# A graph network kernel: the count matrix of its sum layers stored by nodes and read in seven fixed pieces

## What is computed

```
# layer 0: attention with edge features
x = layernorm(x + gat_edge(x, src, dst, edge_attr))
# layers 1, 2, 3: for each node, the mean over its incoming edges
agg = segment_sum(x[src], dst, N)
h   = einsum(agg / max(deg, 1), Wl) + bl + einsum(x, Wr)      # relu between them
# layer 4: a sum with degree weights
h   = relu(segment_sum((x @ W.T)[src] * norm[:, None], dst, N) + b)
# layers 5 and 6: attention layers
```

## Time and profile before

| | |
|---|---|
| median of 3 runs | 3435.23 us (3430.89 to 3437.77) |
| profiled execution, whole time | 3430.6 us |
| its span, first to last instruction | 3428.8 us |
| granted PE clock over the span | 0.892 of full speed |
| busy share of the span | PE 81%, PEld 51%, DVE 53%, ACT 37%, POOL 46% |
| four sum layers, first to last matmul of L745 | about 214 us each |
| building the count matrix | about 53 to 271 us |

### The profile page before, as it was taken

How to read it: one execution, slowest core, us unless ns; L and a number is a source line. 1 busy time by engine, 2 the same in 40 slices (tenths; PEclk the granted TensorE clock), 3 DMA queues, 4 the chain that set the end, 5 groups by cost and what they waited for, 6 DMA issues and landing times.

```text
span 3428.8 us, 52282 instructions
## 1 busy us (share of the span) xinstructions
PE 2781.3 (81%) x13349; PEld 1749.2 (51%) x13350; DVE 1822.2 (53%) x4809; ACT 1263.7 (37%) x3238; POOL 1574.4 (46%) x1469
## 2 busy tenths in 40 slices
PE   6887888888889999999998998477667766767665
PEld 4444555555555555556556455345445534545443
DVE  7996998899952000000003002476666636666665
ACT  3664555555532001001004001644444445444445
POOL 5971666666613004004003100467777537777760
PEclk8997999999989999999999999688888778787885
DMA  6336777777712321321330332345555324455541
GB/s 218 119 113 161 209 208 198 204 207 206 208 41 72 103 76 61 101 86 51 102 95 7 109 104 60 101 134 142 138 141 138 107 84 135 138 141 138 141 116 39
DMA packets 238757, 424.50 MB, mean 124 GB/s; under 512 B 53795, under 2 KB 155095, under 8 KB 238335
## 3 DMA queue, kind: packets, MB, share of 16 engines
q1 hardware_dynamic: 163519, 234.32, 22.5%
q0 software_dynamic: 60544, 173.03, 19.1%
q10 hardware_dynamic: 14400, 13.93, 1.4%
HBM read 381.52 MB, written 39.62 MB: 123 GB/s over the span
## 4 chain that ended last, share of the span: by engine, by line
PE 47%; POOL 17%; DVE 15%; issue 12%; DMA 4%; ACT 3%; DVEq 2%; SPq 0%; ACTq 0%; POOLq 0%
PE ps L745 25%; POOL rows L2138 17%; PE ps L629 5%; PE ps L608 4%; DVE norm L1529 3%; PE ps L997 3%; PE ps L977 3%; DMA rows<-table,src_idx 2%; DVE norm L1352 2%; DVE spread L1519 1%; ACT norm L1168 1%; PE ps L915 1%; PE ps L802 1%; PE ps L595 1%; DVE al L1358 1%
## 5 line engine op out<-in xcount | busy, mean ns | idle before, releaser
L2138 POOL DMA_INDIRECT rows<-table,src_idx x1248 | 1360.0, 1090 | 534.1 <-issue 376.0
L745 PE MATMUL ps<-rows,rT 128*128 128x448 f16 (+1 forms) x3200 | 817.1, 342 | 16.6 <-DMA rows<-adjacency 16.6
L745 PE MATMUL ps<-rows,spread 128*128 128x448 f16 (+1 forms) x1600 | 546.6, 342 | 0.0
L745 PEld LDWEIGHTS ps<-rows,rT 128*128 128x128 bf16 x3200 | 312.1, 98 | 278.2 <-issue 25.5
L2092 POOL CAST rT<-rows 128x1024 bf16<-128x1024 f32 (+1 forms) x28 | 26.6, 950 | 783.9 <-ACT rows L1293 783.9
L1545 DVE TENSOR_TENSOR rows<-ps,norm 128x896 f32<-128x896 f32 (+1 forms) x24 | 24.7, 1027 | 667.4 <-PE ps L745 667.4
L802 PE MATMUL ps<-rows,spread 128*128 128x260 f32 x832 | 283.0, 510 | 62.0 <-DVE rows L1660 62.0
L608 PE MATMUL ps<-rT,spread 128*128 128x272 f32 x832 | 248.9, 423 | 68.4 <-DVE norm L1352 67.5
L802 PE MATMUL ps<-rows,w_roots 128*128 128x260 f32 x832 | 263.8, 480 | 41.3 <-DVE rows L1660 41.1
L802 PEld LDWEIGHTS ps<-rows,spread 128*128 128x128 f32 x832 | 211.2, 261 | 117.6 <-DVE rows L1660 63.4
L1660 DVE TENSOR_TENSOR rows<-rows,ps 128x1024 f32<-128x1024 f32 x208 | 249.1, 1198 | 29.6 <-issue 22.0
(11 more groups left out here) (267 smaller groups left out, 4236.5 us busy)
## 6 DMA issues: line engine op xcount, KB each, us to landing
rows<-adjacency SPq DMA_DIRECT2D x140, 560.0 KB, 3.7
rT<-table SPq DMA_DIRECT2D x316, 136.0 KB, 2.5
spread<-in_tiles SPq DMA_DIRECT2D x104, 256.0 KB, 4.1
rows<-table,src_idx POOLq DMA_INDIRECT x1248
rT<-table ACTq DMA_DIRECT2D x100, 136.0 KB
w_table<-in_tiles SPq DMA_DIRECT2D x52, 256.0 KB
adjacency<-rT SPq DMA_DIRECT2D x4, 2800.0 KB, 11.1
adjacency<-acc SPq DMA_DIRECT2D x3, 2800.0 KB, 11.2
```

The source lines that it names most:

```text
L745: ins = mm(chunk_ps[c % 2][:, f, 0:width], xp[k][:, t, f * P:(f + 1) * P], ring[c][q][:, i, :], start=t == 0 and k == 0, stop=t == ROWS - ...
L2138: pool.indirect_dma_start(src_rows(l, par)[:, k, :], None, tables[l][:, :], bass.IndirectOffsetOnAxis(ap=src_idx[:, g * T + k:g * T + k + ...
```

## The change

The matrix gets one array in HBM, by nodes: 128 partitions x 25 rows x 3584 columns, of which 3136 = 7 x 448 are read. A chunk is stored at its first node's column, an address known only at run time, so chunks overlap in HBM and their stores must land in order: SP waits for the store before. Where a chunk begins, PE carries the shared column from the stage of the chunk before (its column is `link`), so that each column's last writer has the whole sum. The sum layers read seven fixed pieces of columns, 448 each, and DVE no longer needs the first node. DVE's preparation works out chunk starts that leave no gap, and `link`. The last chunk is 232 columns wide instead of 200.

```diff
-WIDTHS = [CC] * (NCK - 1) + [200]
+LAST_CHUNK = 232
+COLUMNS = -(-N // CC) * CC
+PIECES = COLUMNS // CC
...
-        adjacency = nc.dram_tensor("adjacency", (NCK * P, ROWS * CC), F16, kind="Internal").ap()
+        adjacency = nc.dram_tensor("adjacency", (P, ROWS, COLUMNS + CC), F16, kind="Internal").ap()
...
-                if j % CP > 0:
-                    shared = pe.value_load(place[0:1, j:j + 1], min_val=0, max_val=CC)
+                if j > 0:
+                    at_first = j % CP == 0
+                    of_stage = adj_stage[(j - 1) // CP % 2]
+                    shared = pe.value_load(link[0:1, j // CP:j // CP + 1] if at_first else place[0:1, j:j + 1], min_val=0, max_val=CC)
                     pe.wait_ge(adj_copied, 2 * j)
...
-            for c in range(NCK):
-                width = WIDTHS[c]
+            for c in range(PIECES):
...
-                                ins = mm(chunk_ps[c % 2][:, f, 0:width], xp[k][:, t, f * P:(f + 1) * P], ring[c][q][:, i, :],
+                                ins = mm(chunk_ps[c % 2][:, f, :], xp[k][:, t, f * P:(f + 1) * P], ring[q][:, i, :],
...
-                if i == 0:
-                    act.wait_ge(key_used, PACK * (j + 1))
+                if j == 0:
+                    act.wait_ge(key_used, PACK)
                 else:
-                    act.wait_ge(carried, (CP - 1) * c + i)
+                    act.wait_ge(carried, j)
...
-                node = V.value_load(chunk_node[0:1, c:c + 1], min_val=0, max_val=NPAD - width)
...
-                nodes = acc[:, :, bass.ds(node, width)]
-                V.tensor_tensor(nodes, nodes, summed, ALU.add).then_inc(window_added, 1)
+                V.tensor_tensor(acc[:, :, of], acc[:, :, of], summed, ALU.add).then_inc(window_added, 1)
...
+                    width = LAST_CHUNK if c == NCK - 1 else CC
+                    node = sp.value_load(chunk_node[0:1, c:c + 1], min_val=0, max_val=COLUMNS)
                     sp.wait_ge(adj_copied, 2 * (CP * c + PACKS_OF[c]))
-                    to = adjacency[c * P:(c + 1) * P, 0:ROWS * WIDTHS[c]].rearrange("p (h c) -> p h c", h=ROWS)
-                    sp.dma_start(to, adj_stage[c % 2][:, :, 0:WIDTHS[c]]).then_inc(adj_stored[c % 2], 16)
+                    if c > 0:
+                        sp.wait_ge(adj_stored[(c - 1) % 2], 16 * ((c - 1) // 2 + 1))
+                    sp.dma_start(adjacency[:, :, bass.ds(node, width)], adj_stage[c % 2][:, :, 0:width]).then_inc(adj_stored[c % 2], 16)
...
-                        piece = HQ * WIDTHS[c]
-                        sp.dma_start(ring[c][q].rearrange("p h c -> p (h c)"),
-                                     adjacency[c * P:(c + 1) * P, q * piece:(q + 1) * piece]).then_inc(piece_landed[q], 16)
+                        sp.dma_start(ring[q], adjacency[:, q * HQ:(q + 1) * HQ, c * CC:(c + 1) * CC]).then_inc(piece_landed[q], 16)
...
+            V.memset(steps_of[:, :], float(CC))
+            V.tensor_copy(firsts[:, :], pack[:, 0:FULL + 1:CP])
+            ch.then(V.tensor_scalar(more_upto[:, 0:NCK], iota[:, 0:NCK], float(CC), float(COLUMNS - LAST_CHUNK - CC * (NCK - 1)), ALU.mult, ALU.add))
+            ch.then(V.tensor_tensor_scan(starts[:, :], steps_of[:, :], firsts[:, :], -float(CC), ALU.add, ALU.min))
+            ch.then(V.tensor_tensor(starts[:, :], starts[:, :], more_upto[:, 0:NCK], ALU.max))
+            V.tensor_copy(chunk_node[:, :], starts[0:1, :])
+            V.memset(link[:, 0:1], 0.0)
+            ch.then(V.tensor_tensor(firsts[0:1, 1:NCK], firsts[0:1, 1:NCK], starts[0:1, 0:NCK - 1], ALU.subtract))
+            V.tensor_scalar(link[0:1, 1:NCK], firsts[0:1, 1:NCK], 0.0, float(CC), ALU.max, ALU.min)
...
-                ch.then(V.tensor_scalar(chunk_node[:, at].unsqueeze(2), first[:, :, 0:1], NPAD - width, None, ALU.min))
...
+                ch.then(V.scalar_tensor_tensor(unfit[:, of], more_upto[:, of], 0.0, unfit[:, of], ALU.is_lt, ALU.add))
```

More of the change, by code:

```diff
@@ L168, in gnn_program @@
         iota16 = sb("iota16", [P, KEYS], F16)
-        chunk_node = sb("chunk_node", [P, NCK], I32)
+        chunk_node = sb("chunk_node", [1, NCK], I32)
+        starts = sb("starts", [P, NCK])
+        firsts = sb("firsts", [P, NCK])
+        steps_of = sb("steps_of", [P, NCK])
+        link = sb("link", [1, NCK], I32)
         place = sb("place", [1, PACKS], I32)
@@ L215, in gnn_program @@
         xp.append(spread[:, :].bitcast(BF16).rearrange("p (t d) -> p t d", t=ROWS))
-        ring = [[rows[:, q * PIECE:q * PIECE + HQ * w // 2].bitcast(F16).rearrange("p (h c) -> p h c", h=HQ) for q in range(NQ)]
-                for w in WIDTHS]
+        ring = [rows[:, q * PIECE:(q + 1) * PIECE].bitcast(F16).rearrange("p (h c) -> p h c", h=HQ) for q in range(NQ)]
         stage_words = [x[:, 0:ROWS * PITCH // 2].rearrange("p (h c) -> p h c", h=ROWS) for x in (low, early)]
@@ L717, in adjacency_pe @@
                         ins = mm(adj_ps[j % 4][:, h, 0:(end - at) * SPAN], lo, hot[:, at * SPAN:end * SPAN],
-                                 start=k == 0, stop=k == PACK - 1 and j % CP == 0)
+                                 start=k == 0, stop=k == PACK - 1 and j == 0)
                     ins.then_inc(key_used, 1)
-                if j % CP > 0:
-                    shared = pe.value_load(place[0:1, j:j + 1], min_val=0, max_val=CC)
+                if j > 0:
+                    at_first = j % CP == 0
+                    of_stage = adj_stage[(j - 1) // CP % 2]
+                    shared = pe.value_load(link[0:1, j // CP:j // CP + 1] if at_first else place[0:1, j:j + 1], min_val=0, max_val=CC)
                     pe.wait_ge(adj_copied, 2 * j)
@@ L724, in adjacency_pe @@
                         of_row = adj_ps[j % 4][:, h, 0:(end - at) * SPAN].rearrange("p (t n) -> p t n", n=SPAN)
-                        ins = mm(of_row[:, :, 0:1], ident16[:, :], adj_stage[j // CP % 2][:, at:end, bass.ds(shared, 1)],
+                        ins = mm(of_row[:, :, 0:1], ident16[:, :], of_stage[:, at:end, bass.ds(shared, 1)],
                                  start=False, stop=True)
@@ L1533, in sum_dve @@
             mean = l in MEAN_LAYERS
-            before = NCK * (l - 1)
+            before = PIECES * (l - 1)
             if l == MEAN_LAYERS[0]:
                 dve.wait_ge(norm_loaded, 16)
-            for c in range(NCK):
-                width = WIDTHS[c]
-                node = V.value_load(chunk_node[0:1, c:c + 1], min_val=0, max_val=NPAD - width)
-                dve.wait_ge(piece_used, NQ * (NCK * (l - 1) + c + 1))
-                summed = chunk_ps[c % 2][:, :, 0:width]
+            for c in range(PIECES):
+                of = slice(CC * c, CC * (c + 1))
+                dve.wait_ge(piece_used, NQ * (before + c + 1))
+                summed = chunk_ps[c % 2]
                 if before + c > 0:
@@ L1544, in sum_dve @@
                 if mean:
[L1545 to L1548, removed]
-                nodes = acc[:, :, bass.ds(node, width)]
-                V.tensor_tensor(nodes, nodes, summed, ALU.add).then_inc(window_added, 1)
-            dve.wait_ge(window_added, before + NCK)
+                    V.tensor_tensor(weighed[c % 2], summed, norm[:, of].unsqueeze(1).broadcast_to([P, FC, CC]), ALU.mult).then_inc(window_weighed, 1)
+                    dve.wait_ge(window_weighed, PIECES * MEAN_LAYERS.index(l) + c + 1)
+                    summed = weighed[c % 2]
+                V.tensor_tensor(acc[:, :, of], acc[:, :, of], summed, ALU.add).then_inc(window_added, 1)
+            dve.wait_ge(window_added, before + PIECES)
             def window(w):
```

10 lines of the change are left out of this document (5 added, 5 removed).

## The result

The changed kernel takes 3392.09 us (median of four runs, 3389.06 to 3394.05) beside 3435.41 us for the kernel before (four runs, 3430.89 to 3437.77). The ratio is 0.9873, with a 95% interval of 0.9857 to 0.9889: 43.3 us less, 1.3%. The prediction was 3392.5 us, a gain of 42.7. So the total came out; of its terms some did and some did not, and two errors cancelled.

What follows compares the result with a forecast made beforehand. Sum layers were taken as bound by PE's columns at full clock. Terms -51.5 + 3.6 + 1.2 + 0 + 1.5 + 0.3 + 0.75 + 0.4 + 1.0 = -42.7 us gave 3387.9 us profiled, 3392.5 as median, range 3383 to 3409.

Steps and rivals of the forecast that it cites:

- Matmuls: Four sum layers: 150 matmuls of 200 columns removed from each, 12.87 us a layer, -51.5 us in all.
- DVE's last chunk and reading: Sum layers: last chunk's DVE work grows to a full chunk's, +3.6 us; first piece's load in 896-byte rows, +1.2 us.
- the register loads that go stand ahead of waits for PE and give nothing: Sum layers, DVE: removing its register loads was claimed to gain nothing.
- The clock: PE's granted clock after idle time at sum layers' ends: taken as 0, bounds -4.8 to +6.4 us for four layers.
- Preparation: Nine small DVE instructions ahead of `tables_ready` delay the stage's clearing: +1.5 us, bounds 0 and 3.4.
- The carry: Matrix building: carries across chunks cost nothing mid-stage, but one comes before the last packs: +0.3 us, bounds 0 and 0.6.
- Chunk 6's store: Before the edge layer: store to unaligned addresses takes 13 us, of which 0.4 us is not covered (0 to 2.1).
- The count sets the time more than the bytes do: Chunk stores: the reason given for taking 13 us for chunk 6, nearer the aligned rows than 4-byte elements.
- Chunk 7: Before the edge layer: SP's register load and wait +0.75 us, longer uncovered store of 12 us +1.0 us (0 to 4.0).
- Stores at twice the cost: Rival: chunk stores to odd addresses cost twice, about 20 us of the gain go, 3411 us; chance 0.14.
- PE waiting for pieces: Rival, slower: sum layers follow loads of short rows at 6.7 us a piece, +84 us, 3519 us; chance 0.04.
- Packs that don't fit: Rival, no gain: one pack outside the layout runs `further_windows` in each sum layer, giving back all, 3435 us; chance 0.04.

Runs made afterwards that it cites:

- eighth-piece kernel: Changed kernel with an eighth piece of 192 columns, belonging to no node, read and multiplied again in each sum layer: 3429.34 us, ratio 0.9988 to the kernel before.
- two kernels with a last piece of 198 columns: Changed kernel reading six pieces of 488 columns and one of 198: 3384.27 us; the same with DVE writing the tables before the chunk starts: 3383.20 us.
- old kernel with 232 columns: Kernel before the change with a last chunk of 232 columns instead of 200: 3442.34 us in one execution.
- in halves: Changed kernel with each sum-layer piece loaded by two DMAs of 224 columns, 1280 stretches of 448 bytes: 3386.82 us in one execution.
- aligned kernel: Changed kernel with each chunk's start column rounded down to a multiple of 16 (32 bytes) by three more DVE instructions: 3388.31 us, ratio 0.9872 to the kernel before.
- kernel with the tables first: Changed kernel with DVE writing the tables that SP stores before working out chunk starts: 3388.30 us, beside 3392.15 for the changed kernel on the same chip.
- four times the stretches: Changed kernel with each sum-layer piece loaded by four DMAs of 112 columns, 2560 stretches of 224 bytes: 3393.75 us in one execution.

## Why the prediction came out, step by step

The working is the prediction's; what follows is what each term measured in the pair of traces, and in the experiments where the pair doesn't settle it.

**Matmuls: -51.5 predicted, -53.1 measured.** Right within 1.6 us. The difference goes with where in a layer the clock returns. In its two profiles the changed kernel's stretches come in two lengths, 200.2 to 200.5 and 201.7 to 201.8 us. From 4.0 to 6.0 us behind the first matmul the granted clock is 0.87 in layer 1 (200.48 us) and 0.52 in layer 3 (201.70):

```profile
1087.60:1089.60 2.00, 2.00 (x10) 0.96 (x9) 0.00 (x0) 0.00 (x0) 0.00 (x0) 0.87 0.70 187
...
1594.80:1596.80 2.00, 2.00 (x7) 0.83 (x6) 0.00 (x0) 0.00 (x0) 0.00 (x0) 0.52 0.68 172
```

In before three layers are of the longer kind and one is short, in after one is long and three are short. Layers of the same kind differ by some 12.6 us, 50.4 for four, and the rest of the 53.1 is this count. A second profile of the changed kernel has two stretches of each length, 804.2 us in all and so -51.7; over all profiles with these seven pieces it is -51.2 to -53.4.

**DVE's last chunk and reading: +3.6 and +1.2 predicted, +2.4 and +0.4 measured.** Too high. The first is read from a layer's end: how long PE stands still between the last sum matmul and the first of the node stage. Here the chain of before behind layer 1, whose stretch ends at 1289.32 us:

```profile
1289.34 0.05 DVEq L1545
...
1290.06 0.04 DVEq L1550
...
1290.14 0.59 DVE acc L1550
...
1291.43 0.47 issue
...
1292.47 2.04 PE ps L977 x8
```

And that of the eighth-piece kernel, whose last piece is short as well, but which reads no register:

```profile
1076.61 211.17 PE ps L754 x1200
...
1289.68 0.15 issue
...
1290.40 1.13 PE ps L986 x8
```

The same four waits of PE, worked out from the chains (us):

| | layer 1 | layer 2 | layer 3 | layer 4 | sum |
|---|---|---|---|---|---|
| before | 3.15 | 3.15 | 2.64 | 3.45 | 12.4 |
| after | 3.70 | 3.68 | 3.50 | 3.87 | 14.8 |
| eighth piece | 2.62 | 2.61 | 2.43 | 3.33 | 11.0 |

From the eighth-piece kernel to after DVE's last piece grows from 192 to 448 columns, and the waits by 3.8 us: DVE's work reaches PE in full. But from before it is only 2.4, since before pays for something else at the same place. The step that failed is "the register loads that go stand ahead of waits for PE and give nothing". DVE's register work at L1545 and L1550, 0.1 us each with the issue around it, is gone in after, and so are 0.32 us of the "issue" further down (0.47 in before, 0.15 in after and with the eighth piece). In all, before waits 1.4 us longer than the eighth-piece kernel behind DVE work of almost the same length (0.59 and 0.57 us an instruction), and 0.9 and 1.1 us longer than the two kernels with a last piece of 198 columns (11.5 and 11.3 us). And the first piece costs no 0.3 us a layer: PE's four waits for it add up to 16.6 us before, 17.0 after.

The whole time that PE stands still between one layer's matmuls and the next layer's also holds other waits of the node stage. It is the length less PE's busy time in these windows, three each of before, of after, and (the first and the last) of the eighth-piece kernel:

```profile
1289.32:1341.45 52.13, 44.78 (x157) 30.27 (x157) 5.68 (x9) 15.76 (x27) 37.01 (x27) 0.95 0.06 20
1555.70:1607.75 52.05, 44.71 (x156) 30.23 (x157) 5.68 (x9) 15.76 (x27) 37.02 (x27) 0.95 0.06 19
1821.97:1900.27 78.30, 63.45 (x307) 46.49 (x308) 32.22 (x87) 38.41 (x80) 39.55 (x26) 0.97 0.04 14
```

```profile
1284.07:1337.86 53.79, 45.84 (x157) 30.71 (x158) 6.71 (x9) 15.78 (x27) 37.09 (x27) 0.93 0.06 17
1538.05:1590.80 52.75, 44.98 (x157) 30.24 (x157) 6.72 (x9) 15.78 (x27) 37.01 (x26) 0.96 0.06 17
1792.50:1873.04 80.54, 65.52 (x307) 48.63 (x307) 33.28 (x87) 38.46 (x80) 39.85 (x27) 0.94 0.04 13
```

```profile
1287.78:1338.23 50.45, 43.50 (x156) 28.88 (x157) 5.64 (x9) 15.78 (x27) 37.17 (x27) 0.99 0.06 20
...
1813.49:1890.84 77.35, 62.19 (x306) 45.38 (x307) 32.18 (x87) 38.56 (x80) 39.54 (x26) 1.00 0.04 13
```

Before PE stands still for 29.5 us in the three stages (182.48 - 152.94), after for 30.7: +1.2 in this pair. It scatters: 28.4 in the old kernel with 232 columns, 30.5 to 31.6 in five other profiles of kernels that load the same seven pieces, whole or in halves.

**The clock: 0 predicted, +3.4 us in this pair, not shown to be the change's.** The same windows give PE's busy time for the same matmuls: 152.9 us before, 156.3 after, 149.2 with the eighth piece, 151.6 with aligned starts. It goes with the granted clock of the stage, 0.93 to 0.96 in after and 0.99 to 1.00 with the eighth piece. The aligned kernel, where PE stands still as long in the first stage (7.86 us beside after's 7.95), has 0.98 there. Both profiles of the changed kernel give 156.3 or 156.4, the other kernels with the same seven pieces 151.5 to 154.5, the old layout 152.9 and 154.5. So what the clock does there differs between kernels whose instructions in these stages are the same, and why stays open; the bounds of -4.8 to +6.4 held it. One reading behind these bounds was off: the slow stretch at the end of layer 1 in before is 3.0 us long and not 2.4 (0.50 from the first matmul at 1292.47, and a mean of 0.64 from 1294.3 to 1296.0, so the clock returns at 1295.5). With it they would be about -6 and +5.

**Preparation: +1.5 predicted, +2.18 measured.** Right in place: 1.71 us until the stores of the tables are issued, 0.48 in their DMA. In other kernels with the same preparation the clearing starts between 60.09 and 61.26 us, and at 59.90 in the old kernel with 232 columns, so of this about one microsecond is scatter. What was overlooked is that SP's own queue stands one microsecond behind, as the kernel with the tables first showed.

**The carry: +0.3 predicted, not to be told from zero.** From the clearing to chunk 6's store it is 200.5 us before, 201.8 after; but 201.8 as well in the old kernel with 232 columns, and 200.8 in the aligned one. The 1.3 us of this pair count below as the stretch behind the clearing.

**Chunk 6's store: +0.4 predicted, +2.0 measured.** The size was off: 13 us were taken, 14.99 came, and SP reached the spans 15.01 us after the issue instead of 13.03. The bound, 15.1 us and +2.1, held it. "The count sets the time more than the bytes do" made the aligned rows look nearer than they were.

**Chunk 7: +1.75 predicted, -1.0 measured.** The sign was wrong. The register load and the issues behind it cost 0.67 us, near the 0.75 predicted. But the store lands in 8.4 us instead of 11.1, and the load of `in_tiles` beside it takes 3.90 us instead of 5.96 (3.5 to 4.2 in the other kernels with the changed building, 5.07 in the old one with 232 columns); the hot matrix then takes 0.43 more. The bounds of this store, 0 to 4 us, left out a gain without a reason. The nearest row was taken for an ordinary store of 400-byte rows, when the layout of these rows, one behind the other, was what made it slow.

These two errors, +1.6 and -2.7, cancel in part, and the preparation (+0.7) and the stretch behind the clearing (+1.0) make up the rest: the way to the edge layer was to be 3.95 us longer and is 4.45. That this sum came out is luck.

**Layer 0 and the attention layers: 0 predicted, +4.2 and +2.3 in this pair.** From the hot matrix to the first sum matmul it is 776.9 us before and 781.1 after; with PE busy 673.7 and 680.0 us for the same instructions. Over the other profiles of the changed building it is 772.7 to 782.7, and 778.1 in the old one with 232 columns, so no shift shows. Behind the last sum layer it is 1315.5 us before and 1317.8 after, 1316.4 in the old kernel with 232 columns and in the second profile of the changed one, so none shows there either.

Put together: -53.1 + 1.2 + 3.4 + 4.45 + 4.2 + 2.3 = -37.5 us, the difference of the two spans. The prediction's -42.7 was worked out for the profiled execution, 3387.9 us, and that came at 3393.1, with 9.9 us more from the clock, layer 0 and the attention layers, for which no shift is shown. To the median it went by taking the 4.6 us between before's profiled execution and its median for the changed kernel too. The changed kernel's profiled execution lies 1.0 us above its median instead. So that 3392.5 met the median of 3392.1 within half a microsecond is in part luck as well; the columns, its main term, are not.

**The rivals.** Stores at twice the cost: no, 29% more for chunk 6 (14.99 against 11.66). PE waiting for pieces: no, not at four times the stretches. Packs that don't fit: no, PE has 4200 matmuls in L751 and none in the loop behind it (L759, L767).

## What to carry to other kernels

Where PE bounds a stage at full clock, columns that overlap between pieces are paid in full; a layout by place that has each column once returns them at its price per column, and putting the work back is the test of it. What a layer does behind its last piece is paid once a layer, so the short piece belongs at the end. Price loads by loads and stores by stores, and give a store's bounds both signs when its layout in HBM changes, not only its bytes.

## What the hardware showed that was not expected

- Single stores of 3200 rows of 896 bytes take 10.2 to 12.9 us where each row starts at a multiple of 32 bytes, and 13.0 to 16.0 us where the starts are other even addresses (chunk 6's: 11.7 to 12.0 against 13.9 to 16.0). A start at a multiple of 16 is not enough (chunk 4's: 13.0 to 14.0).
- Stores of 3200 short rows take 11.1 and 10.6 us where the rows touch in HBM (400 and 464 bytes), and 7.9 to 8.8 us where they lie 7168 bytes apart, with starts that are multiples of 16 bytes or of 32. Rows of 896 bytes that touch show no such surplus.
- Loads of 560 KB in 128, 640, 1280 and 2560 stretches keep the DMA engines busy for 0.32, 0.34, 0.36 and 0.46 of a sum layer's middle: down to 448 bytes a stretch they go nearly by bytes, not by count.
- The same matmuls behind the same idle time of PE (3.7 us) were granted 0.93 in both profiles of the changed kernel and 0.98 to 0.99 in four others (45.8 against 43.5 us for the first node stage), without an edit that reaches them.
